# Two normalisations from VectorE to ScalarE, and the five scan buffers split 2 and 3 in place of 3 and 2

## The reference, cut to what matters

```python
def _layernorm(x, axis=-1, eps=1e-05):
    m = jnp.mean(x, axis=axis, keepdims=True)
    v = jnp.var(x, axis=axis, keepdims=True)
    return (x - m) / jnp.sqrt(v + eps)
...
    x = L0_attn_x
    xn = _layernorm(x, axis=-1)
    s = _L0_attn_ref(xn, ...)             # softmax(q k / 128, diagonal masked) v
    g = _silu(_L0_ffn_ref(xn, ...))       # top 2 of 8 experts, 128 -> 256 -> 128
    x = x + s * g
    xn = _layernorm(x, axis=-1)
    s = _L1_attn_ref(xn, ...)             # rmsnorm, in_proj, conv, silu, selective scan, out_proj
    g = _silu(_L1_ffn_ref(xn, ...))       # one of 8 experts, layernorm * gamma + beta, 128 -> 512 -> 128
    x = x + s * g
...
        def _selective_scan(u, delta, A, Bm, Cm, D):
            def step(s, inp):
                d_t, B_t, C_t, u_t = inp
                dA = jnp.exp(d_t[..., None] * A)
                dBu = d_t[..., None] * B_t[:, None, :] * u_t[..., None]
                s = s * dA + dBu
                y = jnp.einsum('bds,bs->bd', s, C_t)
                return (s, y)
```

## Time and profile before

| | |
|---|---|
| median of 3 runs | 982.8 us (982.41 to 982.96) |
| the profiled execution | 983.75 us, its span 981.9 us |
| busy PE, DVE | 855.8, 810.0 us |
| busy ACT, POOL | 608.9, 587.6 us |
| share of the chain that ended last | PE 55%, DVE 21%, issue 9%, POOL 8%, ACT 5% |

### The profile page before, as it was taken

One profiled execution on the slowest core, in us unless ns is written; L12 is line 12 of the kernel. 1 busy time (PEld: TensorE's weight loads), 2 busy tenths in 40 slices (PEclk: granted clock), 3 DMA queues, 4 the chain that ended last, 5 costly groups with the idle time before them and its releaser, 6 DMA issues.

```text
span 981.9 us, 15767 instructions
## 1 busy us (share of the span) xinstructions
PE 855.8 (87%) x4624; PEld 582.9 (59%) x4624; DVE 810.0 (82%) x1542; ACT 608.9 (62%) x1315; POOL 587.6 (60%) x524
## 2 busy tenths in 40 slices
PE   5997897999699978999799969999799977684995
PEld 3773475766467745766477736776477645452762
DVE  4244537999989889999999998998999989886995
ACT  3424644868467766778477765778477765574661
POOL 0010202848856695848766694848765697669665
PEclk9977699999899999999999998999999989796998
DMA  7200103224323334324323243225322234324542
GB/s 263 88 0 1 44 12 105 72 80 97 115 65 90 96 94 128 76 76 121 94 89 93 75 115 99 76 78 131 100 85 79 77 101 138 98 72 113 156 132 51
DMA packets 79428, 90.27 MB, mean 92 GB/s; under 512 B 8450, under 2 KB 49906, under 8 KB 78834
## 3 DMA queue, kind: packets, MB, share of 16 engines
q1 hardware_dynamic: 77298, 85.07, 29.5%
q0 software_dynamic: 2048, 4.20, 1.5%
HBM read 52.96 MB, written 13.04 MB: 67 GB/s over the span
## 4 chain that ended last, share of the span: by engine, by line
PE 55%; DVE 21%; issue 9%; POOL 8%; ACT 5%; SPq 1%; DMA 1%; DVEq 0%; POOLq 0%
PE work L823 10%; PE work L829 9%; DVE st L1303 7%; PE work L854 5%; PE yacc L888 5%; PE work L864 5%; PE work L752 3%; POOL st L1470 3%; PE work L773 3%; DVE b_row L1296 2%; PE work L796 2%; PE work L743 2%; PE b_row L877 2%; ACT prob L944 1%; PE work L725 1%
## 5 line engine op out<-in xcount | busy, mean ns | idle before, releaser
L1470 POOL TENSOR_TENSOR st<-st,Cs 128x512 f32<-128x512 f32 x249 | 316.8, 1278 | 178.1 <-DVE st L1303 162.9
L944 ACT ACTIVATE dA<-delta,Aneg 128x512 f32<-128x512 f32 x256 | 175.5, 723 | 20.6 <-POOL du L1431 10.7
L888 PE MATMUL yacc<-st,w_ident 128*128 128x512 f32 x256 | 143.6, 650 | 19.5 <-POOL st L1470 19.1
L1303 DVE TENSOR_TENSOR_SCAN st<-dA,dbu 128x512 f32<-128x512 f32 x128 | 154.7, 1209 | 1.4 <-PE yacc L888 0.6
L1303 DVE TENSOR_TENSOR_SCAN st<-dA,b_row 128x512 f32<-128x512 f32 x123 | 148.7, 1209 | 3.1 <-POOL y L1477 3.1
L829 PEld LDWEIGHTS work<-w_w2a,hid 128*128 128x128 f32 x1024 | 124.3, 195 | 29.4 <-issue 13.0
L944 ACT ACTIVATE hsT<-work,hs 128x128 f32<-128x128 f32 x352 | 99.7, 370 | 61.0 <-PE work L854 60.3
L823 PE MATMUL work<-xnT,w_w1a 128*128 128x512 f32 x256 | 134.5, 615 | 0.7 <-ACT dt L944 0.7
L1477 POOL TENSOR_TENSOR y<-y,st 128x512 f32<-128x512 f32 x105 | 133.2, 1269 | 3.0
L829 PE MATMUL work<-w_w2a,hid 128*128 128x128 f32 x1024 | 127.3, 279 | 5.2 <-ACT hid L944 5.2
L944 ACT ACTIVATE hid<-work,w_b1a 128x512 f32<-128x512 f32 x128 | 87.9, 688 | 66.5 <-PE work L823 62.1
(11 more groups left out here) (187 smaller groups left out, 1315.0 us busy)
## 6 DMA issues: line engine op xcount, KB each, us to landing
Cs<-c_dram SPq DMA_DIRECT2D x128, 256.0 KB
hs<-w_w1f SPq DMA_DIRECT2D x88, 258.0 KB, 2.4
xs_in<-xs_dram SPq DMA_DIRECT2D x16, 256.0 KB
ys_dram<-ys SPq DMA_DIRECT2D x16, 256.0 KB, 2.2
w_w1f<-in_w1f_dram SPq DMA_DIRECT2D x1, 2064.0 KB, 7.7
x_in<-in_x_dram SPq DMA_DIRECT2D x8, 256.0 KB
w_w2f<-in_w2f_dram SPq DMA_DIRECT2D x1, 2048.0 KB, 12.8
kept_dram<-x_tok SPq DMA_DIRECT2D x8, 256.0 KB, 2.4
```

The lines of the kernel that those rows point to most:

```text
L888: mm(yacc[:], ident[:], state(s), start=False, stop=(n == NS - 1)).then_inc(sig["y_sum0"], 1)
L944: return nc.scalar.activation(out, in_, func, **k)
L1303: V.tensor_tensor_scan(state(s), dA[:, s % DECAYS], (dbu0, rows_bank(n, b))[h][:], 0.0, ALU.mult, ALU.add).then_inc(sig["scan"], 1)
L1470: G.tensor_tensor(state(s), state(s), Cs[:, b.of(NS, n) % C_BUFS], ALU.mult).then_inc(sig["P"], 1)
```

## The change

Both normalisations, `xn` and `xm`, move from VectorE to ScalarE, as `Identity` with a scale and a bias per token. The bias is minus mean times rstd. POOL makes it with two more operations of 128x4 in each `ln0` and `ln1` (16 in all, so 32 operations more). The step `xm` on ACT then holds eight instructions of 128x128, its own four and the four of the rmsnorm. DVE's `silu` waits for ACT's `xm` of the batch before, since that still reads `x_tok`.

```diff
+                elif name == "xn":
+                    act.wait_ge(sig["rstd0"], b.of(1, 1))
+                    for t in range(NT):
+                        last = go(xn_tok[:, t], x_in[:, par, t], ACT.Identity, scale=rstd[:, t:t + 1], bias=shift[:, t:t + 1])
+                    last.then_inc(sig["xn0"], 1)
                 elif name == "xm":
+                    act.wait_ge(sig["rstd1"], b.of(1, 1))
+                    since(act, sig["opx"], b.of(1, -1))
+                    for t in range(NT):
+                        last = go(xn1_tok[:, par, t], x_tok[:, t], ACT.Identity, scale=rstd1[:, t:t + 1], bias=shift1[:, t:t + 1])
+                    last.then_inc(sig["xn1"], 1)
...
-                elif name == "xn":
-                    dve.wait_ge(sig["rstd0"], b.of(1, 1))
-                    for t in range(NT):
-                        last = V.tensor_scalar(xn_tok[:, t], x_in[:, par, t], mv[:, t, 0:1], rstd[:, t:t + 1],
-                                               ALU.subtract, ALU.mult)
-                    last.then_inc(sig["xn0"], 1)
...
+                    since(dve, sig["xn1"], b.of(1))
...
-                elif name == "xm":
-                    dve.wait_ge(sig["rstd1"], b.of(1, 1))
-                    for t in range(NT):
-                        last = V.tensor_scalar(xn1_tok[:, par, t], x_tok[:, t], mv1[:, t, 0:1], rstd1[:, t:t + 1],
-                                               ALU.subtract, ALU.mult)
-                    last.then_inc(sig["xn1"], 1)
...
-                    last = G.tensor_tensor(rstd_k[:], ve_k[:], neghalf[:], ALU.pow)
+                    lk(g, G.tensor_tensor(rstd_k[:], ve_k[:], neghalf[:], ALU.pow))
+                    lk(g, G.tensor_tensor(ve_k[:], mv_k[:, :, 0], rstd_k[:], ALU.mult))
+                    last = G.tensor_tensor((shift if k == "0" else shift1)[:], zeros[:], ve_k[:], ALU.subtract)
```

Two of the five buffers now serve half 0 and three serve half 1, and the whole table of times, lags and banks is another (290 rows and `OWN`), of which these rows show the form:

```diff
-STATES = ((0, 1, 2) * 5 + (1,), (3, 4) * (NS // 2))
+STATES = ((0, 1) * (NS // 2), (2, 3, 4) * 5 + (3,))
...
-    ("P", "pe", 0, -1.02692, 2, -3, 0, None),
+    ("P", "pe", 0, -0.68385, 5, 1, -2, None),
-    ("S", "a", 11, 0.84075, 4, 3, 1, None),
+    ("S", "a", 11, 0.78586, 8, -1, -2, None),
```

More of the change, by code:

```diff
@@ L325 @@
     ("A", 0): (
[4 rows of a table removed]
[4 rows of a table added]
     ),
     ("H", 0): (
-        -1.11900, -1.08467, -1.01476, -0.83547, -0.90068, -0.85797, -0.89443, -0.84069, -0.83471, -0.83140, -0.82978, -0.62226,
-        -0.81859, -0.79895, -0.81765, -0.90515, -0.81371, -0.74442, -0.61163, -0.90703, -0.69090, -0.71827, -0.58703, -0.54773,
-        -0.50916, -0.42023, -1.08490, -1.30874,
+        -1.29082, -1.28624, -1.05644, -1.02231, -0.92108, -0.84312, -0.84823, -0.84234, -0.83820, -0.82752, -0.80187, 0.20339,
+        -0.79211, -0.74792, -0.76619, -0.87880, -0.75613, -0.71939, -0.56181, -0.76544, -0.59528, -0.87078, -0.82098, -0.51752,
+        -0.50327, -0.57376, -0.68166, -0.85111,
     ),
     ("A", 1): (
[4 rows of a table removed]
[4 rows of a table added]
     ),
@@ L496, in build @@
         rstd2 = sb("rstd2", [128, NT])
+        shift, shift1 = sb("shift", [128, NT]), sb("shift1", [128, NT])
+        zeros = sb("zeros", [128, NT])
         xn1_tok = sb("xn1_tok", [128, 2, NT, D])
@@ L1397, in _ @@
             V.memset(eps[:], EPS)
+            V.memset(zeros[:], 0.0)
             V.memset(fe[:], 0.0)
```

## The result

The changed kernel takes 998.8 us (median; 997.6 to 1001.9) against 982.6 us of the kernel before: ratio 1.018, 95% interval 1.0164 to 1.0195. It is 16.2 us slower. The prediction was slower by 7.6 us (990.4), with a range of 969 to 1001. The direction was right and the time lies in the range, but the size is more than twice what was forecast. The profiled execution took 1001.86 us, 3 us above its median, so differences of two or three microseconds between two traces mean little here.

The account below looks back on a forecast made before the run. TensorE was taken to bound most of a steady period, VectorE its last stretch. Terms -1.2 + 9.2 + 2.0 + 1.6 - 0.7 - 3.3 = +7.6 us gave 991.35 for a profiled run, 990.4 for the median, range 969 to 1001.

Parts of the forecast that it names:

- window of batch 6: Window without stage A: cheaper xm replacement gains 1.7 us, half of 3.1 us of scan waits goes; together -3.3 us.
- What bounds the kernel: Steady period: TensorE bounds the first 77.50 us, VectorE the last 25.6 us, where alone VectorE's relief can pay.
- One-column products: Prologue: products move from a hidden place onto the chain, 12.9 us less gains of the new order: +9.2 us.
- Start: Start of the program: xn on ScalarE waits behind bqs, so TensorE's first transposes start at about 10.9: +2.0 us.
- First `ln1`: First second layernorm: longer GpSimd and ScalarE work, and x1T ahead of xi on TensorE: +1.6 us.
- Scans of batch 0: Start of batch 0's scans: VectorE is freed of xn and its wait, so scans start earlier: -0.7 us.
- Steady periods: Batches 0 to 5: +1.9 for early sums, -1.4 for xn, -0.7 for the logarithm's place: -0.2 us each, -1.2 in all.
- Rival 1: VectorE sets the pace of the steady periods, so its relief returns 15.6 to 31.8 us: 958.6 to 974.8; chance 0.20.
- Rival 2: Steady periods: ScalarE's xn waits for GpSimd's longer ln0, delaying evictions and TensorE: +9.8 us on the forecast, 1000.2; chance 0.14.
- Rival 3: Prologue: one-column products hidden (981.2 to 977.5 us) or run at the fast clock rate (984.4 us); chance 0.16.

Follow-up runs that it names:

- after_pe_early: Changed kernel with the one-column products back in their old place, ahead of the first transposes of stage H: 985.7 us, ratio 1.0039.
- before_xm_act: Kernel before with only the second normalisation (xm) and its two small GpSimd operations moved, xm to ScalarE: 983.3 us, ratio 1.0011.
- before_dve_less: Kernel before with VectorE's accumulations of dense experts 6 and 7 made for one of four token tiles in batches 2 to 7: 984.2 us, ratio 1.0020.
- before_act_norms_later: Kernel before with the normalisations alone on ScalarE, xn just ahead of xT, behind the routed experts' first evictions: 988.6 us, ratio 1.0073.
- before_pe_late: Kernel before with only the one-column products moved, to between the values of batch 1 and the second delta product: 994.1 us, ratio 1.0128.
- after_pe_early_xn0: Changed kernel with the one-column products at their old place and, for batch 0 alone, xn on VectorE: 983.4 us, ratio 1.0009.
- before_act_norms: Kernel before with the normalisations alone on ScalarE, xn ahead of the routed experts' evictions: 1027.0 us, ratio 1.0461.
- before_pe_warm: Kernel before with the one-column products moved into stage A of batch 1, where its granted clock was 1.00: 994.8 us, ratio 1.0119.
- before_pool_less: Kernel before with GpSimd's products with C of steps 28 and 29 on 4 columns of 512 in batches 0 to 6: 973.2 us, ratio 0.9919.

## Why the prediction was right or wrong

The step that failed is the term for the window of batch 6: -3.3 us were forecast, and with the last window it was +2.8, in the trace of the changed kernel and in that of after_pe_early. These 6 us are most of the 8.6 that are missing. The rest of the sum was near, in part by luck.

- **Window of batch 6, -3.3.** I let 1.7 + 0.56 us take the place of VectorE's 3.97 on the way to the transposes. From VectorE's mean (826.80 and 844.07) to the first transposes it took 11.06 us before and 10.85 us after: 0.2 us gained in place of 1.7. The changed kernel there:

```profile
849.82 1.65 ACT L946 ACTIVATE xn_tok<-x_tok,shift,rstd 128x128 f32<-128x128 f32 x4 [1.76 <-POOL rstd L1432]
854.92 0.60 PE L767 MATMUL work<-w_ident,hx 128*128 128x128 f32 x4
```

  GpSimd began `ln1` 1.5 us behind the mean, after two products with C, and `hx` was ready at 852.8. But TensorE's list has a sum (L890) ahead of the transposes, which waited 2.55 us for GpSimd's next product, itself behind the longer `ln1`, and products of the routed experts. VectorE's own scans did come nearer: 17.3 us late at the tenth scan of that batch, 13.6 at the eleventh. By GpSimd's first put that was gone (15.4), and the window ended over GpSimd, as it did in the kernel before: from its first put to its last add 32.5 us with 30.3 busy, against 31.9 and 30.1, with `endt` ahead of it on the chain. The waits for GpSimd's sums, of which I counted half, all lay in this window and went (3.1 us to 0.2), but they weren't what ended it. Scans of half 0 now wait 9.0 us in the whole run for TensorE's sums, where it was 1.4, and the sum has no term for that.
- **What bounds the kernel.** Right for the first stretch: VectorE's 4.0 us of `xm` there are worth nothing (before_xm_act). Wrong for the third. I read VectorE's 23.37 of 25.6 us busy and its place in the chain of one period as the bound. Relief of VectorE gave nothing (before_dve_less, before_act_norms_later), relief of GpSimd 8.4 us, though it was busy only 20.46 us there. In the trace of before two of the first six windows ended over GpSimd, and the four that ended over VectorE had lost 1.26 us each to the clock.
- **One-column products, +9.2.** Mechanism right, and near in size. From the first transposes of stage H to the first scan of batch 0 it took 78.3 us before, 73.0 in after_pe_early and 86.2 in the changed kernel: +13.1 for the products (12.9 less 0.8 by the sum, 12.2 by before_pe_late) and -5.2 for the other moves (-2.9 by the sum), so +7.9. The clock at the new place was near 0.50, as forecast. But it had been 1.00 just ahead of the products.
- **Start, +2.0**: 1.9 in the trace besides the later load, 2.3 by after_pe_early_xn0. **First `ln1`, +1.6**: from the last dense product's accumulation to the first transposes of stage H it took 12.46 us in place of 11.39, so +1.1. Besides, stage A of batch 0 became 1.2 us longer, which the prediction didn't count.
- **Scans of batch 0, -0.7**: none of it came. The scans were 12.7 us late at the first and 13.6 us late at the last.
- **Steady periods, -0.2 each**: +0.3 in the trace of the changed kernel (13.6 us at the end of batch 0, 15.3 us at the end of batch 5), -0.5 in that of after_pe_early (+2.2 and -0.3). The size held, partly by luck. "I give back all of the 1.43 us" takes the relief of VectorE as worth the same in either order. In the old order it is worth nothing, in the new one both normalisations are worth 22 to 24 us, since that order without them is so much slower.
- **Rivals.** Rival 1 (VectorE sets the pace) is refuted for the kernel before, by three runs. (Half of 5.5 less 0.2 in six periods is 15.3 us, and not 15.6.) Rival 2 (ScalarE late behind GpSimd) didn't come in the changed kernel, which has `xn` behind the evictions, but it is real: 45 us in before_act_norms. Rival 3 is refuted twice: by place, and by rate, since the products did not keep the full clock even where they began at it.

The sum of 16.2 us is then: 13.1 for the one-column products, 2.3 for the first `xn`, and 0.8 for all the rest, which the ratio of after_pe_early_xn0 to before (1.0009, 0.9 us) can't tell from zero. For that rest the prediction had -6.5. It is a balance of parts that are large one by one: in the new order the old split costs 10 us, and the normalisations back on VectorE 22 to 24.

## What to carry to other kernels

A near tie of two engines in a stretch is not settled by the chain of one period. Look at every period's chain, and at the granted clock beside it. Then take one microsecond off each engine in turn, and off both. A step moved to another engine gains on the way to its consumer only what the consumer's own list lets through: look at what stands ahead of it there. Work that an order hides in an idle engine (here 64 small products beside a normalisation) is the first thing to look for when an order is rewritten, since its full price comes due at once. When an order, a choice of buffers and a choice of engines were found together, test them together: the new order with the old buffers (1008.9 us) or with the old engines (1022.4) was worse than both kernels.

## What the runs showed of the hardware

Sixty-four products of one column in a row, with TensorE busy by the record, took the granted clock from 1.00 to 0.50 while they ran behind dense products (rows 6, before_pe_warm), and it did not rise while they ran where it was already at 0.50 (before_pe_late). The 128x512 products behind them ran at the low clock for some microseconds more (3.76 us for four in before_pe_warm, for 1.98). After one and the same wait of TensorE of 1.91 us the clock fell in four of six windows of the kernel before and in none of before_pool_less. A scan of 128x8 on VectorE took 0.17 us by itself and 0.77 us beside a product of GpSimd (tensor_tensor, 128x512), with which it ended. An Identity on ScalarE with scale and bias per token took 1.63 to 1.68 us for four of 128x128, against 1.28 us with a scale alone. The Trainium skill's figure for a further pointer operand ("ScalarE: Activation LUTs", What ACT_TABLE_LOAD costs) agrees with that.
